# Scaling and masking of the retention scores: two passes on two engines replaced by one VectorE operation

## The reference

```python
qkv = x @ W_qkv
q, k, v = split_heads(...)                       # 16 heads of 64
decay[t, s] = gamma ** (t - s) if t >= s else 0  # gamma = 1 - 2 ** (-5 - head)
ret = einsum('bhtd,bhsd->bhts', q, k) * decay
inner = einsum('bhts,bhsd->bhtd', ret, v)
cross = einsum('bhtd,hde->bhte', q, past_kv) * 1024
r = inner + cross                                # then normalised over the whole sequence
```

## Time and profile before

| what | us |
|---|---|
| median of 2 runs | 7595.64 |
| lowest and highest of them | 7582.94, 7608.33 |
| the profiled execution | 7600.34 |
| span of its slowest core (core 7) | 7598.7 |

### The profile page before, as it was taken

How to read it: one execution, slowest core, us unless ns; L and a number is a source line. 1 busy time by engine, 2 the same in 40 slices (tenths; PEclk the granted TensorE clock), 3 DMA queues, 4 the chain that set the end, 5 groups by cost and what they waited for, 6 DMA issues and landing times.

```text
span 7598.7 us, 72810 instructions; the slowest of 8 cores (7521.3 to 7598.7 us)
## 1 busy us (share of the span) xinstructions
PE 4040.2 (53%) x18936; PEld 1987.4 (26%) x18936; DVE 2822.8 (37%) x10391; ACT 1629.0 (21%) x3693; POOL 86.2 (1%) x102
## 2 busy tenths in 40 slices
PE   4545454345665665574555454543456656655645
PEld 1222221222322322232222222212223223222322
DVE  4223223463334333433442222234543343334334
ACT  2121213112311321222022212131123112211220
POOL 0000000000000000000000000000000000000000
PEclk8656565567776776786656565555677767767866
DMA  2100000000000000000021000000000000000001
GB/s 54 17 5 5 9 1 0 9 11 11 8 4 11 8 7 8 11 4 1 39 57 10 5 9 5 1 0 9 11 11 8 6 10 11 4 8 11 4 1 45
DMA packets 114460, 84.89 MB, mean 11 GB/s; under 512 B 55663, under 2 KB 105202, under 8 KB 114066
## 3 DMA queue, kind: packets, MB, share of 16 engines
q0 software_dynamic: 101536, 45.49, 5.0%
q1 hardware_dynamic: 12530, 34.75, 1.3%
HBM read 108.93 MB, written 16.78 MB: 17 GB/s over the span
## 4 chain that ended last, share of the span: by engine, by line
PE 46%; DVE 28%; issue 14%; ACT 10%; DVEq 1%; DMA 1%; ACTq 0%; SPq 0%; POOL 0%; POOLq 0%
PE PA L987 13%; ACT ETb L1109 5%; PE PA L1219 4%; DVE gac L1024 3%; PE PA L1118 3%; DVE ztk L1183 3%; PE PBF L1197 3%; ACT stc L633 3%; DVE zp L1202 2%; PE PB L556 2%; DVE xT L1226 2%; PE PA L534 2%; PE PA L644 2%; PE PB L1103 2%; PE PB L628 2%
## 5 line engine op out<-in xcount | busy, mean ns | idle before, releaser
L987 PE MATMUL PA<-wb,xnT 128*128 128x320 bf16 x6144 | 1012.8, 335 | 214.9 <-ACT q5t L993 211.4
L1109 ACT ACTIVATE ETb<-PB,smc 128x512 bf16<-128x512 f32 x1024 | 661.4, 685 | 1294.2 <-PE PB L1103 1285.3
L987 PEld LDWEIGHTS PA<-wb,xnT 128*128 128x128 bf16 x6144 | 659.6, 108 | 550.5 <-issue 222.6
L993 ACT CAST q5t<-PA 128x320 bf16<-128x320 f32 x768 | 326.4, 426 | 1897.0 <-PE PA L987 1553.0
L1197 PE MATMUL PBF<-identb,ztk 128*128 128x128 bf16 (+1 forms) x768 | 203.2, 265 | 818.0 <-DVE ztk L1183 570.7
L1118 PE MATMUL PA<-ETb,vag 128*128 128x512 bf16 x1024 | 415.0, 405 | 205.5 <-ACT ETb L1109 195.8
L1219 PE MATMUL PA<-zp,wo_hat 128*128 128x512 bf16 x1280 | 355.8, 433 | 223.8 <-DVE xT L1226 220.0
L1024 DVE SCALAR_TENSOR_TENSOR gac<-q5t,ggt,gac 128x64 f32<-128x64 bf16 x2304 | 455.0, 274 | 0.0
L1103 PE MATMUL PB<-qfT,kfT 128*128 128x512 bf16 x1024 | 417.0, 418 | 7.5 <-DVE smc L1089 6.6
L644 PE MATMUL PA<-stc,vtok 128*64 128x128 bf16 x512 | 146.1, 285 | 481.8 <-DVE stc L639 481.8
L639 DVE TENSOR_TENSOR stc<-stc,dmasks 128x128 bf16<-128x128 bf16 x512 | 115.1, 225 | 666.1 <-ACT stc L633 666.1
(11 more groups left out here) (230 smaller groups left out, 5239.2 us busy)
## 6 DMA issues: line engine op xcount, KB each, us to landing
wb<-Wkv POOLq DMA_DIRECT2D x32, 640.0 KB, 6.7
xs<-x SPq DMA_DIRECT2D x32, 512.0 KB
y<-ys SPq DMA_DIRECT2D x32, 512.0 KB
wb<-Wq POOLq DMA_DIRECT2D x16, 640.0 KB, 6.8
wqt<-Wqkv POOLq DMA_DIRECT2D x16, 256.0 KB, 4.4
wkt<-Wqkv POOLq DMA_DIRECT2D x16, 256.0 KB, 6.0
wvt<-Wqkv POOLq DMA_DIRECT2D x16, 256.0 KB, 6.5
wo_hat<-Wo_hat POOLq DMA_DIRECT2D x1, 1280.0 KB, 14.9
```

The source lines that it names most:

```text
L987: mmq = pr.emit("tensor", (lambda aa, tt, bk, pa2: lambda te: te.matmul(PA[:, bk * 512:bk * 512 + 320], xnT[:, aa * T + tt * 128:aa * T + ...
L993: ev_pj[t] = pr.emit("scalar", (lambda tt, bk: lambda sc: sc.copy(out=q5tok[:, tt * 320:(tt + 1) * 320], in_=PA[:, bk * 512:bk * 512 + 320 ...
L1109: ex_prev[j] = pr.emit("scalar", (lambda jj, s2, p2, p_: lambda sc: sc.activation(out=ET[:, s2 * 512:(s2 + 1) * 512], in_=PB[:, p2 * 512:( ...
```

## The change

ACT's pass L633 and DVE's pass L639 are replaced by one DVE operation. It reads the scores from PSUM, multiplies by the per-partition value of `gkcols` and then by the mask, and writes `st_ch`. Its waits are those of the former ACT pass; L644 and L659 wait for it as they waited for L639. Nothing else differs.

```diff
-                    sc_ev = pr.emit("scalar", (lambda cc2, hq, bk, sl: lambda sc: sc.activation(
+                    ev = pr.emit("vector", (lambda cc2, hq, bk, sl: lambda v: v.scalar_tensor_tensor(
                         out=st_ch[:, sl * 128:(sl + 1) * 128],
-                        in_=PB[:, bk * 512:bk * 512 + 128], func=AF.Identity,
-                        scale=gkcols[:, hq * 16 + cc2:hq * 16 + cc2 + 1]))(
-                            c, h, bank, (2 * c + hh) % 4),
+                        in0=PB[:, bk * 512:bk * 512 + 128],
+                        scalar=gkcols[:, hq * 16 + cc2:hq * 16 + cc2 + 1],
+                        in1=dmasks[:, 0:128],
+                        op0=OP.mult, op1=OP.mult))(c, h, bank, (2 * c + hh) % 4),
                         waits=[mmst, sv_last])
-                    ev = pr.emit("vector", (lambda sl: lambda v: v.tensor_tensor(
-                        out=st_ch[:, sl * 128:(sl + 1) * 128],
-                        in0=st_ch[:, sl * 128:(sl + 1) * 128],
-                        in1=dmasks[:, 0:128], op=OP.mult))((2 * c + hh) % 4),
-                        waits=[sc_ev])
```

## The result

| | before | changed |
|---|---|---|
| median, us | 7583.27 (10 runs) | 7440.56 (11 runs) |
| lowest, highest | 7534.95, 7608.33 | 7397.34, 7508.65 |
| ratio, 95% interval | | 0.9807 (0.9773 to 0.9842) |

The changed kernel is 1.9% faster; whether it is by more than 2% the interval leaves open. The ratio is of fast runs alone, so it is not the quotient of the medians: it leaves out the run of 7508.65 us, in which one die was over 1% longer than the other at a lower clock, while the median counts it. The forecast of 7465 us was 0.9822 of its base, and the range of 7420 to 7500 holds the median.

The account below looks back on a forecast made before the run. The retention chunk loop's serial chain of waits was taken as the path, with no engine full. 169.0 us saved minus 33.6 lost gave 135.4, taking 7600.3 to 7465 us; range 7420 to 7500.

Parts of the forecast that it names:

- The chunk loop is a chain with nothing beside it: Retention stage, L628 to the next L628: serial waits of 2.38 us a chunk, about 1219 us or 16% of the span.
- The fused operation takes 351 ns: New DVE operation at L633: 291 ns as a plain PSUM copy plus 60 for the per-partition scalar; bounds 291 and 484.
- Saved at L644: 169.0 us: L628's end to L644's start falls from 0.941 to 0.611 us, saving 0.330 us in each of 512 chunks.
- One more wait on DVE, 33.6 us lost: State addition L666 gets a second wait, on ACT's cast, issued after PE's: 0.07 us in each of 480 runs.
- The cheaper cases: Rival, chance 0.24: per-partition scalar free (30.7 us more, 7434) or second wait absorbed (33.6 us more, 7431); both 7401.
- The clock in the loop: Rival, chance 0.05: the denser chunk loop is granted a higher PE clock, 102 us more gain, 7363 at most.
- The total: Whole kernel: 135.4 us off the profiled 7600.3 gives 7465 us, 1.8% less; forecast's chance 0.58.
- The projections and the FFN as before: Outside the retention loop: the trace after should show the projections and whole FFN unchanged.
- within 2%: Whole kernel: change under 152 us, border near 7444; forecast and dearer case fall within it, 0.68.

Follow-up runs that it names:

- scores ahead: Changed kernel with swapped waits, chunks alternating between two PSUM banks and the next chunk's score matmul issued ahead of L640: ratio 0.9412, 7152.9 us.
- fused operation ahead: The scores ahead kernel with, on DVE, the fused operation of chunk c+1 also issued ahead of chunk c's state addition: ratio 0.9351, 7112.7 us.

## Why the prediction was right

- *The chunk loop is a chain with nothing beside it.* Right. All of what the operation lost shows up at PE, and nothing else became last.
- *The fused operation takes 351 ns.* Measured 350. The parts hold one by one: 292 ns without the per-partition scalar (predicted 291), 58 ns for the scalar (predicted 60, between the 49 and 64 of the earlier trace rows). The value for the isolated instruction was the right one to lean on.
- *Saved at L644: 169.0 us.* Measured 170.3.
- *One more wait on DVE, 33.6 us lost.* Measured 33.5. The kernel before with one more wait alone shows the same 261.6 us, and the changed kernel with the cast's wait first 226.6. The rule "the semaphore costs nothing extra here", of the Trainium skill's page "VectorE: DVE Perf Modes", section "The DRAIN you can't avoid", was measured there with copies of one engine, and it does not carry over to a wait behind the late one: here that costs 0.07 us each, and ahead of the late one nothing.
- *Rivals.* The cheaper cases fell with the 350 ns and the 33.5 us. The clock in the loop did not rise: it was granted 0.50 before and after, and matmul L628 took 263 ns before and 264 after. The Trainium skill's estimate of 258 ns (same page, section "The TRN2 errata") for 128 columns from PSUM is 34 ns below the 292 measured without the scalar.
- *The total.* The sum was made against one execution of 7600.3 us. The median of ten runs is 7583.3, so the same 135.4 us give 7447.9, and 7440.6 was measured. The 24 us between 7465 and 7440.6 are thus 17 us of base and 7 us that the interval does not resolve.
- *The projections and the FFN as before.* Not so in the profiles: the FFN's largest matmul group took 335 ns before and 328 after. The prediction had warned that the cores' spread could move the total by some tens of us; its cause, the granted clock of one die, it did not have. That the profiled executions differ by 199 us and not 137 is luck of the two executions.

The chance for "within 2%" was 0.68, and the step of 136.8 us in the rows is 1.8% of 7583.3; the interval of the ratio, 0.9773 to 0.9842, does not settle on which side of 2% it lies.

## What to carry to other kernels

When a pass on one engine is taken out, look for the waits it made on behalf of later instructions: a wait that had been covered comes back, and it costs where it stands. Put the wait that is satisfied last at the end of the list; the early ones then run in its shade. And before shortening the links of a serial chain, ask why it is serial: fusing two passes brought 1.9%, letting the chunks take turns on two PSUM banks (together with the better order of the waits, some 0.5%) brought 4 to 5% more.

## What the runs showed of the hardware

- On DVE a wait already satisfied costs 0.07 us when it is issued behind the late one, each (33.5, 33.5 and 34.6 us for 480), and nothing ahead of it.
- A per-partition scalar costs this SCALAR_TENSOR_TENSOR of 128 columns 58 ns an instruction (350 against 292); a second tensor read from SBUF beside one in PSUM costs nothing (292 ns against 291 for the copy).
- Two DVE instructions without a wait between them overlapped by a third of the first: 0.14 us from start to start, with the first lasting 0.21 (state addition and fused operation, scores ahead).
- The two dies of one chip differed by 70.7 us in one execution of one program, at mean clocks of 0.672 and 0.688. The slower one had a granted clock of 0.81 in 90 to 162 of 800 windows of 2 us, the other in 2 at most. This hides steps below 1% in the times of the slowest core, while the idle times in the rows repeat to some 2 us and the shortest die medians agree with them to some 6 us.
- The chunk loop was granted 0.50 in every kernel looked at, with PE busy from 15.08 of 37 us (before) to 13.01 of 20 us (fused operation ahead).
